# Interleaving the output projection's matmuls with the probability transposes of head 13 in an attention loop

## The reference

```python
q = _w8a8_linear(x, wq, bq)            # x is layer-normed; operands rounded to 8-bit integers
k = cond @ wk.T + bk
v = cond @ wv.T + bv
scores = einsum('bnhd,blhd->bhnl', q, k) / sqrt(32) + mask
attn = softmax(scores)
o = einsum('bhnl,bhld->bnhd', attn, v)
out = _w8a8_linear(o, wo, bo)          # the output projection: quantized o times quantized wo
x = x + out
x = x + moe_ffn(layernorm(x))          # 8 experts, top 2
```

## Time and profile before

| | us |
|---|---|
| three timed runs: median (lowest to highest) | 1606.87 (1602.88 to 1607.51) |
| the profiled execution | 1609.71 |
| its span from first to last instruction | 1608.0 |
| attention's steady iteration, mean of two neighbours (481.26 to 545.80) | 32.27 |
| PE busy over the span | 1494.6 (93%) |
| DVE, ACT, POOL busy | 897.5, 884.0, 660.6 |

### The profile page before, as it was taken

How to read it: one execution, slowest core, us unless ns; L and a number is a source line. 1 busy time by engine, 2 the same in 40 slices (tenths; PEclk the granted TensorE clock), 3 DMA queues, 4 the chain that set the end, 5 groups by cost and what they waited for, 6 DMA issues and landing times. The chain is left out here.

```text
span 1608.0 us, 40123 instructions
## 1 busy us (share of the span) xinstructions
PE 1494.6 (93%) x11594; PEld 1317.6 (82%) x11595; DVE 897.5 (56%) x2365; ACT 884.0 (55%) x2097; POOL 660.6 (41%) x671
## 2 busy tenths in 40 slices
PE   2899999999999999999999999984399999999896
PEld 2788888888888888888888888873299999999895
DVE  6557666766676667666766676654632222222221
ACT  2467667677777776777677767761033333333232
POOL 4233334333443234323432343323555555656453
PEclk9999999999999999999999999985599999999998
DMA  5567777677767776777677767654537776666643
GB/s 173 145 170 196 209 200 197 179 228 205 194 178 226 202 196 179 225 205 196 178 225 201 200 179 222 185 142 141 160 68 186 182 175 134 148 154 125 160 77 48
DMA packets 220124, 281.09 MB, mean 175 GB/s; under 512 B 83568, under 2 KB 164976, under 8 KB 220080
## 3 DMA queue, kind: packets, MB, share of 16 engines
q1 hardware_dynamic: 203952, 247.24, 54.3%
q0 software_dynamic: 16128, 33.30, 11.6%
HBM read 118.31 MB, written 66.17 MB: 115 GB/s over the span
## 5 line engine op out<-in xcount | busy, mean ns | idle before, releaser
L464 DVE CUSTOM_DVE_ANT_0 probs<-score,neg_mask 112x375 f32<-112x375 f32 x512 | 279.7, 546 | 254.8 <-PE score L555 251.5
L392 ACT ACTIVATE probs<-probs,neg_max 112x375 f32<-112x375 f32 x512 | 312.3, 610 | 197.2 <-DVE neg_max L464 191.7
L563 PE MATMUL turn<-ident,probs 112*125 112x112 f32 x1536 | 264.8, 282 | 2.8 <-ACT probs L392 2.5
L385 ACT ACTIVATE probs_t<-turn 125x336 f32<-125x336 f32 x512 | 226.0, 441 | 71.6 <-PE turn L563 70.6
L563 PEld LDWEIGHTS turn<-ident,probs 112*125 112x125 f32 x1536 | 227.2, 190 | 36.4 <-issue 14.4
L555 PE MATMUL score<-k_stack,q_stack 96*112 96x376 f32 x512 | 209.4, 409 | 8.5 <-DMA q_stack<-q_lo 6.2
L591 PE MATMUL proj<-ctx_hi,wk_hi 128*128 128x376 f32 x512 | 176.0, 344 | 1.9 <-PEq L29 1.1
L591 PE MATMUL proj<-ctx_lo,wk_hi 128*128 128x376 f32 x512 | 172.0, 336 | 0.0
L591 PE MATMUL proj<-ctx_hi,wk_lo 128*128 128x376 f32 x512 | 171.7, 335 | 0.0
L1032 DVE TENSOR_TENSOR a_lo<-a_ps,a_hi 128x384 fp32r<-128x384 f32 x63 | 35.1, 557 | 243.7 <-ACT a_hi L1007 243.7
L596 PE MATMUL proj<-wv_hi,ctx_hi 128*125 128x512 f32 x384 | 151.8, 395 | 0.0
(11 more groups left out here) (198 smaller groups left out, 3393.9 us busy)
## 6 DMA issues: line engine op xcount, KB each, us to landing
k_stack<-k_hi SPq DMA_DIRECT2D x512, 94.0 KB, 2.2
k_stack<-k_lo SPq DMA_DIRECT2D x256, 94.0 KB, 2.2
ctx_stage<-ctx_t SPq DMA_DIRECT2D x32, 750.0 KB, 5.0
q_stack<-q_hi SPq DMA_DIRECT2D x256, 56.0 KB, 2.0
w_raw<-gate_up_t SPq DMA_DIRECT2D x32, 352.0 KB, 3.1
gate_up_dram_hi<-w_hi SPq DMA_DIRECT2D x32, 352.0 KB, 4.8
gate_up_dram_lo<-w_raw SPq DMA_DIRECT2D x32, 352.0 KB, 5.2
gate_up_hi<-gate_up_dram_hi SPq DMA_DIRECT2D x16, 704.0 KB, 4.9
```

What stands on the lines that cost most here:

```text
L385: act.activation(probs_t[:, h % RING_T, :, :], turn[h % 2][0:LC, 0:LT * N].rearrange("p (l n) -> p l n", l=LT), ACT.Copy).then_inc(turned_ ...
L392: act.activation(probs[:, h % DS, :], probs[:, h % DS, :], ACT.Exp, bias=neg_max[:, par % 2, h:h + 1], scale=-1.0, accum_out=total[:, par ...
L464: dve.tensor_tensor_reduce(probs[:, h % DS, :], score[h % 2][0:N, 0:L], neg_mask[:, p, :], 1.0, BIG, ALU.add, ALU.min, neg_max[:, p, h:h + ...
L563: mm = pe.transpose(turn[h % 2][0:LC, l * N:(l + 1) * N], probs[:, h % DS, l * LC:(l + 1) * LC], W["ident"][0:N, 0:N])
```

## The change

The batch's four output-projection matmuls move ahead of the score of head 15. One stands ahead of each of the three transposes of head 13, and the fourth behind the last of them. The SBUF tile `o_int_t` grows from 112 to 128 columns for each of its four pieces; DVE zeroes the added 16 columns once, before the first iteration, and PE waits for that once. The four matmuls now load 128 columns instead of 112 and write all 128 partitions of `misc`. In the one iteration that has no heads of its own, the four stay together. The core of the diff:

```diff
-        o_int, o_int_t = sb("o_int", [N, C], BF16), sb("o_int_t", [128, KT, N], BF16)
+        o_int, o_int_t = sb("o_int", [N, C], BF16), sb("o_int_t", [128, KT, 128], BF16)
...
-                        dve.tensor_scalar(o_int_t[:, :, :], misc16[:, 0:KT * N].rearrange("p (t n) -> p t n", t=KT),
+                        dve.tensor_scalar(o_int_t[:, :, 0:N], misc16[:, 0:KT * N].rearrange("p (t n) -> p t n", t=KT),
...
+            dve.memset(o_int_t[:, :, N:128], 0.0).then_inc(o_int_padded, 1)
...
-            def turn_probs(b, h):
+            def turn_probs(b, h, before=None):
                 k = b * H + h
                 need(pe, softmaxed, k + 1)
                 need(pe, turned_out, k - 1)
                 for l in range(LT):
+                    if before:
+                        before(l)
                     mm = pe.transpose(turn[h % 2][0:LC, l * N:(l + 1) * N], probs[:, h % DS, l * LC:(l + 1) * LC],
                                       W["ident"][0:N, 0:N])
                 mm.then_inc(turned, 1)
+
+            def weigh_out(t):
+                return pe.matmul(misc[:, :], o_int_t[:, t, :], W["wo_int"][:, t, :], start=(t == 0), stop=(t == KT - 1))
...
-                    if h >= 2 and has_a:
+                    if h == 15 and has_m:
+                        need(pe, o_out, 3 * m + 2)
+                    if h == 15 and has_m and has_a:
+                        turn_probs(it, h - 2, weigh_out)
+                        weigh_out(KT - 1).then_inc(o_made, 1)
+                    elif h >= 2 and has_a:
                         turn_probs(it, h - 2)
...
-                    if h == 15 and has_m:
-                        need(pe, o_out, 3 * m + 2)
+                    if h == 15 and has_m and not has_a:
                         for t in range(KT):
-                            mm = pe.matmul(misc[0:N, :], o_int_t[:, t, :], W["wo_int"][:, t, :], start=(t == 0), stop=(t == KT - 1))
+                            mm = weigh_out(t)
                         mm.then_inc(o_made, 1)
...
+            pe.wait_ge(o_int_padded, 1)
             iterations(pe, body)
```

More of the change, by code:

```diff
@@ L236, in attention @@
         x1_stored, h2_stored = sem("x1_stored"), sem("h2_stored")
+        o_int_padded = sem("o_int_padded")
         w_in, w_hi_made, w_lo_made, w_stored = sem("w_in"), sem("w_hi_made"), sem("w_lo_made"), sem("w_stored")
```

## The result

The changed kernel takes 1625.33 us (median of 4 runs, 1621.94 to 1630.1) against 1607.12. The ratio is 1.0122, with a 95% interval from 1.0091 to 1.0152. It is slower, as forecast, but by more: the medians differ by 18.2 us where 12.8 was forecast. The median itself, 1625.33, lies just inside the forecast range, but 1.0122 times the time before is 1626.7, just beyond its upper end of 1626.

A forecast was written before the change was run, and what follows sets the result against it. PE was taken to bound the kernel, busy 1002.77 of 1012 us in attention's steady part. Steady iterations 11.3, iteration 30 0.7 and iteration 31 0.8 summed to 12.8 us: 1606.9 + 12.8 = 1620 us, range 1612 to 1626.

The forecast's parts named there:

- the idle that ends on the exponential: PE ahead of the transposes of head 15: about 0.8 us of waiting, where there was 0.35.
- the clock of the steady part: Attention's steady iterations: the granted clock stays at 1.00, the 2.4 GHz level.
- I take 0.05 for the slot: Between two projection matmuls: a transpose's stream and the next piece's load take 0.05 us, upper bound 0.105.
- 0.39 and 0.52 an iteration: Steady iterations: transposes of head 15 start 0.39 us later, or 0.52 past the loop's branch.
- PE's own work shrinks by 0.17: Step 15: transposes of head 14 start 1.18 us after it begins instead of 1.35, saving 0.17 an iteration.
- 0.22 and not 0.27: DVE at head 15: a mask step waiting only for its score begins 0.27 us after the score ends.
- the slower slot: Between projection matmuls: 0.105 us instead of 0.05, 4.5 us more in all, 1624 us; chance 14%.
- my 0.7: Iteration 30, followed by one without projections: transposes of head 15 start at 1064.74 instead of 1064.00, 0.7 us.
- my 0.8: Iteration 31, projection matmuls counted at half clock: score falls back by up to 1.7 us, part slack, 0.8 taken.
- A load that does not hide under the matmul ahead: Step 15: loads of three transposes and the score lie open, 11 us more, 1631 us; chance 2%.
- given back by a later wait: Later PE waits absorb 8 us of the 13, time about 1607 us; chance 8%.
- the saving alone: Head 15's exponential comes before PE reaches its transposes: 5.3 us saved over 31 iterations, 1601.6 us; chance 6%.

The follow-up runs named there:

- the plain block ahead: kernel before, its four projection matmuls moved as one block, unpadded and not interleaved, ahead of the score of head 15: 1625.63 us, ratio 1.0106.
- the run with 56 rows: changed kernel, transposes of head 13 taking only the first 56 of 112 token rows: 1646.68 us, ratio 1.025.
- the kernel with both repairs: changed kernel, score of head 15 put ahead of the interleaved group and two large quantizing operations moved to step 2: 1605.51 us, ratio 0.9982.
- quantizing later: kernel before, two large quantizing operations of the next input moved from step 14 to step 2 of the next iteration: 1602.5 us, ratio 0.9966.

## Why the prediction was right and where it was wrong

**The mechanism.** The late score of head 15 through mask step and exponential to the transposes of head 15 is shown: with the score first the loss is gone, with a plain block ahead of it the loss is whole, with two matmuls ahead it is what the slack leaves. The direction, the idle that ends on the exponential (0.88 where 0.8 was forecast), and the clock of the steady part (1.00) came as written. That DVE's quantizing was the bound before, and gave the slack, is shown from both sides: by removing it there (a gain of 4.3 us, 4.5 expected from the waits) and in the changed kernel (nothing in the steady iteration).

**The step that failed** is "I take 0.05 for the slot". It measured 0.10. Behind it stands the reading that the identity streaming past needs less time than the load, for which no row was given. Transposes in a row stand 0.103 apart (median, kernel before), and an interleaved one takes a slot of 0.099: the stream is nearly as long as the distance that I put down to the load. I read 0.05 from bf16 transposes of the earlier trace rows, and named the fp32 transpose's bare stream as what could make it 0.105, with 14%; it is that. So the mask step came at 1.73 instead of 1.61, the transposes of head 15 0.12 us later than forecast, 0.52 and 0.64 instead of 0.39 and 0.52 an iteration. 13 x 0.52 + 12 x 0.64 = 14.4 instead of 11.3, and the trace has 15.2. With it fell the second claim, that PE's own work shrinks by 0.17: it did not shrink, and with the chain out of the way interleaving still bought nothing.

A second term was off the other way, by luck. The score comes 0.17 later than forecast, but a mask step comes 0.22 and not 0.27 behind the end of the score's record, which took some of it back. The earlier trace rows show a 0.27; of 400 mask steps in the middle of that trace 226 came at 0.22 and 72 at 0.28. The time that I gave for the slower slot, 1624, is 1.3 us from the measured median, but it rests on that term and on those of the next paragraph too.

**The ends of the attention and the experts.** I had 1.5 us for iterations 30 and 31. In iteration 30 the chain did what it does elsewhere: the transposes of head 15 start 3.07 us into step 15 instead of 2.21, which is 0.86 for my 0.7. But the stretch up to step 14 of iteration 31 grew by 2.2. The granted clock falls there in both kernels (0.79 and 0.76 over the stretch), and over the thirteen traces the stretch takes between 26.1 and 29.7 us; the plain block ahead, with the same chain, takes 27.62. What of the 2.2 is clock and what is chain stays open. Behind it my 0.8 is not seen (33.72 and 33.77). The experts, whose code is the same in all kernels, take 446.0 to 449.4 us from one trace to another, and the first stretch 247.7 to 255.0. So single executions differ by several us outside the steady iterations, also where the code is the same. That is also why the ratio of 1.0122 need not be what the steady iterations alone give (1 + 15/1607 = 1.0093), and why 1625.33, 1622.81 and 1621.59 stand beside the same 32.8 to 32.9 us a steady iteration.

**The other rivals.** A load that does not hide under the matmul ahead is refuted for 112 rows: the transposes follow the projection matmuls by 0.22, their stream alone. The rule of the Trainium skill in "TensorE: Matmul & The Clock Gate", Part 3, by which only a load for another row group overlaps, does not hold here: the transposes' and the projection's loads span all four groups, and it is the run with 56 rows, with fewer groups, in which the overlap goes (0.32 and 0.24). Fewer groups alone can't be the reason: the score's load has 96 rows and still hides under the 512-column matmul ahead (0.23 from start to start, 510.67 to 510.90 in the kernel with both repairs). Why 56 rows lose the overlap stays open. Nothing was given back by a later wait: the places lose 0.52 and 0.64, the steady iteration 0.60. In the changed kernel's steady iterations PE came to the transposes of head 15 ahead of the exponential's end; the saving alone never counted.

## What to carry to other kernels

Before short matmuls are interleaved with long ones, ask what the short one's own stream takes. Interleaving leaves that stream in place, so it pays only where the slot that is left (0.10 here) is clearly less than the distance of two short ones in a row (0.103 here). A price read from another data type (0.05, bf16) did not carry over. Before work is moved ahead of an instruction, ask which chain that instruction starts: the score was the first link of the one chain that PE waits for. The same reading shows where to gain: PE's idle of 0.2 us named ACT, ACT's named DVE, and DVE was doing work (`x_int`, written by 514.72) that PE took up only at 528.0, some 13 us later.

## What the runs showed of the hardware that was not expected

- The fp32 transposes stream at 0.9 ns a column (112 columns 0.10 us in the changed kernel, 72 columns 0.065), while the score's 376 columns, whose operands are of type fp32r, take 0.17 (510.90 to 511.07 with both repairs), under 0.5 ns each, at the same granted clock of 1.00.
- A transpose of 56 rows between matmuls of 128 rows is followed after 0.24 us and comes 0.32 after the matmul ahead; with 72 rows it is 0.065 and 0.22.
- A load of 112 bf16 columns has a record of 130 ns and one of 128 has 98, but with either the next matmul starts 0.065 us behind a transpose of 72 rows.
- A mask step that waits for its score mostly starts 0.22 us behind the end of the score's record, whether that record is 0.33 us long (both repairs), 0.40 (quantizing later) or 0.53 (the changed kernel).
